# First layer of a fused convolution kernel on sums and differences of columns w and w+256, with a row transform 128 columns wide

## What is computed

```python
x = x + _L0_conv_ref(_gn(x), w_real, w_imag, b_real, b_imag)
x = x + _L1_conv_ref(_gn(x))
x = x + _L2_conv_ref(_gn(x), W)
x = x + _L3_conv_ref(_gn(x), weight)

def _L0_conv_ref(x, w_real, w_imag, b_real, b_imag):
    X = jnp.fft.rfftn(x, axes=(-2, -1), norm='backward')
    Xr, Xi = (jnp.real(X), jnp.imag(X))
    ...
    Yr = _rconv(Xr, wr) - _rconv(Xi, wi) + b_real[:, None, None]   # 3x3
    Yi = _rconv(Xr, wi) + _rconv(Xi, wr) + b_imag[:, None, None]
    return jnp.fft.irfftn(lax.complex(Yr, Yi), axes=(-2, -1), norm='backward')
def _L1_conv_ref(uvs):          # per channel: row sums, a 0/1 gate per row
    u, v = jnp.split(uvs, 2, axis=1)
    left_gate = relu(sign(einsum('bkmd,bkd->bkm', u, v.sum(axis=2))))[..., None]
    right_gate = relu(sign(einsum('bknd,bkd->bkn', v, u.sum(axis=2))))[..., None]
    return jnp.concatenate([left_gate * u, right_gate * v], axis=1)
```

## Time and profile before

| | |
|---|---|
| median of 3 runs | 4616.99 us (4616.7 to 4618.75) |
| profiled execution, its own time | 4618.31 us |
| its span | 4616.5 us |
| TensorE busy | 4235.7 us (92%), mean granted clock 0.959 of full speed |
| VectorE busy | 2761.5 us (60%) |
| ACT busy | 2639.8 us (57%) |
| GpSimd busy | 3.5 us in 22 instructions |

### The profile page before, as it was taken

How to read it: one execution, slowest core, us unless ns; L and a number is a source line. 1 busy time by engine, 2 the same in 40 slices (tenths; PEclk the granted TensorE clock), 3 DMA queues, 4 the chain that set the end, 5 groups by cost and what they waited for, 6 DMA issues and landing times.

```text
span 4616.5 us, 172871 instructions
## 1 busy us (share of the span) xinstructions
PE 4235.7 (92%) x60064; PEld 2295.8 (50%) x60064; DVE 2761.5 (60%) x9972; ACT 2639.8 (57%) x7597; POOL 3.5 (0%) x22
## 2 busy tenths in 40 slices
PE   4999899989999899998999989999899989888785
PEld 1555435555455544555445543555436553455441
DVE  1777727775377744777257771776727775377730
ACT  4456665547555565555655566555565556544453
POOL 0000000000000000000000000000000000000000
PEclk8999899999999999999999999999899999999987
DMA  7444666647665576665656566564766647544476
GB/s 203 110 120 114 166 162 175 175 132 183 159 177 175 139 171 163 176 175 147 162 160 176 168 160 165 159 175 145 170 157 177 177 135 183 144 120 124 107 183 183
DMA packets 437852, 732.96 MB, mean 159 GB/s; under 512 B 42544, under 2 KB 109296, under 8 KB 437232
## 3 DMA queue, kind: packets, MB, share of 16 engines
q1 hardware_dynamic: 416112, 688.51, 54.2%
q10 hardware_dynamic: 21248, 37.76, 4.1%
HBM read 323.98 MB, written 134.22 MB: 99 GB/s over the span
## 4 chain that ended last, share of the span: by engine, by line
PE 85%; DMA 6%; DVE 3%; issue 3%; SPq 2%; ACT 1%; ACTq 0%; DVEq 0%
PE ps L1358 26%; PE ps L1276 20%; PE ps L1261 19%; PE ps L1269 6%; PE ps L1285 5%; PE ps L1135 5%; DMA shared<-x 3%; DMA out<-x 2%; PE ps L1383 1%; DMA x<-x 1%; PE ps L1208 1%; PE ps L1181 1%; PE ps L1182 0%; SPq L401 0%; DVE shared L911 0%
## 5 line engine op out<-in xcount | busy, mean ns | idle before, releaser
L1358 PE MATMUL ps<-x,conv_s 64*32 64x512 f32 x12288 | 1398.5, 610 | 88.8 <-DMA shared<-x 83.6
L1358 PE MATMUL ps<-shared,conv_s 64*32 64x512 f32 x12288 | 1407.1, 609 | 0.0
L645 ACT ACTIVATE x<-ps,vec 128x256 f32 (+1 forms) x1024 | 491.3, 496 | 998.1 <-PE ps L1276 998.1
L1276 PE MATMUL ps<-hil,shared 128*128 128x256 f32 x4096 | 993.6, 386 | 0.0
L1276 PEld LDWEIGHTS ps<-hil,shared 128*128 128x128 f32 x4096 | 740.4, 190 | 273.8 <-issue 194.1
L911 DVE SCALAR_TENSOR_TENSOR shared<-xin,trig 128x256 f32<-128x256 f32 x2048 | 822.2, 440 | 57.3
L1358 PEld LDWEIGHTS ps<-x,conv_s 64*32 64x32 f32 x12288 | 428.0, 108 | 646.1 <-issue 581.6
L720 ACT ACTIVATE x<-ps,vec 64x512 f32<-64x512 f32 (+1 forms) x768 | 526.3, 685 | 340.7 <-PE ps L1358 331.1
L1261 PE MATMUL ps<-shared 32*32 32x512 f32 x16384 | 657.9, 602 | 0.0
L923 DVE COPY vsb<-ps 128x512 f32<-128x512 f32 x512 | 329.9, 686 | 545.9 <-PE ps L1261 545.9
L1358 PEld LDWEIGHTS ps<-shared,conv_s 64*32 64x32 f32 x12288 | 501.4, 108 | 196.6 <-issue 157.4
(11 more groups left out here) (175 smaller groups left out, 3366.5 us busy)
## 6 DMA issues: line engine op xcount, KB each, us to landing
shared<-x SPq DMA_DIRECT2D x680, 256.0 KB, 4.8
xin<-x SPq DMA_DIRECT2D x512, 256.0 KB
out<-x SPq DMA_DIRECT2D x512, 256.0 KB
shared<-x SPq DMA_DIRECT2D x128, 768.0 KB, 7.0
shared<-x SPq DMA_DIRECT2D x496, 128.0 KB, 3.5
shared<-t_strip SPq DMA_DIRECT2D x512, 96.0 KB, 3.7
shared<-x ACTq DMA_DIRECT2D x128, 256.0 KB, 4.3
x<-x SPq DMA_DIRECT2D x64, 256.0 KB, 9.1
```

The lines of the kernel that those rows point to most:

```text
L645: ins = nc.scalar.activation(split_in(strip_of(s))[:, q, :], split_in(ps[:, bank, :])[:, q, :], ACT.Identity, bias=v1(MEAN), accum_out=sum ...
L1276: mm = pe.matmul(split_in(ps[:, BY + 2 * odd + e, :])[:, int(q < 2), :], xt[:, e, q, :], hil[:, q, 0:HALF], start=False, stop=True, skip_g ...
L1358: mm = pe.matmul(ps[TM * cg:TM * cg + TM, banks[k], :], conv_s[rows, kw, kind, :], of, start=(kw == 0), stop=(kw == TAPS - 1), skip_group_ ...
```

## The change

- `xin` is split by GpSimd, behind the load: the upper 256 columns become x[w]-x[w+256], the lower ones x[w]+x[w+256], less twice the mean. VectorE no longer takes the mean off; it waits for `x_split` in place of the load. Cos and sin change sign from w to w+256, so a product by them turns sums into differences and back: planes are now four pieces of 128 columns with sums and two of 256 without.
- All of the first layer's values stay sums and differences, to `x1`. The row transform takes them to themselves: each of its four products covers 128 columns (`hil_s`). `over_half` keeps the old transform for the column sums.
- ACT evicts the lower half in two pieces of 128 columns, even and odd, with sums, and the upper half in one of 256 without. ACT makes the copy of V of the second strip, VectorE that of the first.
- The gates bring the columns back: GpSimd makes gate times the lower half plus offset (`lifts`, four slots), VectorE adds and subtracts gate times the upper half (`gate_low`, `gate_high`).
- Tables and `u` are scaled by one half; `u`, the column sums and the setup get their own sums and differences; sums and squares are doubled on the way to the gates.

```diff
-    hil_t = np.zeros((P, 4, HW_))
+    hil_t = np.zeros((P, HIL))
     for k in range(4):
         rows = split[k * P:(k + 1) * P]
         cols = n[1::2] if k < 2 else n[::2]
-        hil_t[:, k, :HALF] = hil[rows][:, cols]
-        hil_t[:, k, HALF:] = g[rows]
+        if k % 2 == 0:
+            hil_t[:, HALF * (k // 2):HALF * (k // 2 + 1)] = hil[rows][:, cols]
+            for half, sign in enumerate((1, -1)):
+                hil_t[:, HIL_S + P * (k + half):HIL_S + P * (k + half + 1)] = hil[rows][:, cols[:P]] + sign * hil[rows][:, cols[P:]]
+        hil_t[:, HIL_G + NG * k:HIL_G + NG * (k + 1)] = g[rows]
...
-            strip[s, h + 3 * C + ch, p] = row_out == 0
+                strip[s, h + C * k + ch, p] = 0.5 * f[row_out]
+            strip[s, h + 3 * C + ch, p] = 0.5 * (row_out == 0)
...
-    eye_mix[p, 0, AXS, p % TM] = 1.0
+    eye_mix[p, 0, AXS, p % TM] = 0.5
...
-DVE_B = 6
+DVE_B = 7
+POOL_B = 2
+LIFT_FREE = 4
...
-        hil = sb("hil", P, 4, HW_)
+        hil = sb("hil", P, HIL)
+        hil_lo = hil[:, 0:N].rearrange("p (k w) -> p k w", k=2)
+        hil_g = hil[:, HIL_G:HIL_S].rearrange("p (k g) -> p k g", k=4)
+        hil_s = hil[:, HIL_S:HIL].rearrange("p (k w) -> p k w", k=4)
...
+        lifts = [a[:, HALF * h:HALF * (h + 1)] for a in (colv, vs) for h in range(2)]
+        junk_d = xt[:, 1].rearrange("p a b -> p (a b)")
...
+            pool.sem_inc(gated, LIFT_FREE)
             with pool.Fori(0, B) as i:
+
+                pool.wait_ge(v_scaled, i + 1)
+                pool.sem_inc(s_pad, 1)
+                with pool.Fori(0, STRIPS // UNROLL) as j:
+                    for k in range(UNROLL):
+                        b = Steps(pool, p_steps, (i * STRIPS + j * UNROLL + k) * POOL_B)
+                        low, high = (halves(xin[:, k, :])[:, h, :] for h in range(2))
+                        pool.wait_ge(x_loaded[k], (i * (STRIPS // UNROLL) + j + 1) * 16)
+                        b.then(nc.gpsimd.tensor_tensor(high, low, high, ALU.subtract))
+                        pool.sem_inc(s_pad, 1)
+                        b.then(nc.gpsimd.tensor_scalar(low, low, v1(MEAN), 2.0, ALU.subtract, ALU.mult))
+                        nc.gpsimd.tensor_tensor(low, low, high, ALU.subtract).then_inc(x_split, 1)
...
+                pool.wait_ge(v_gates, i + 1)
+                for n in range(STRIPS):
+                    s = STRIPS - 1 - n
+                    pool.wait_ge(gated, gd(i, n - LIFT_FREE + 1))
+                    pool.sem_inc(s_pad, 1)
+                    for q in range(2):
+                        ins = nc.gpsimd.tensor_scalar(split_in(lifts[n % LIFT_FREE])[:, q, :], signs(x1[:, s, 1:1 + N])[:, 0, q, :], cols[:, 4, s:s + 1],
+                                                      gate_b[:, q, s:s + 1], ALU.mult, ALU.add)
+                    ins.then_inc(lifted, 1)
...
-                        ins = nc.scalar.activation(split_in(strip_of(s))[:, q, :], split_in(ps[:, bank, :])[:, q, :], ACT.Identity, bias=v1(MEAN),
-                                                   accum_out=sums[:, q, bass.ds(s, 1)])
-                    ins.then_inc(y_evicted, 1)
+                        nc.scalar.activation(signs(strip_of(s))[:, 0, q, :], signs(ps[:, bank, :])[:, 0, q, :], ACT.Identity, bias=v1(MEAN),
+                                             accum_out=sums[:, q, bass.ds(s, 1)])
+                    nc.scalar.activation(halves(strip_of(s))[:, 1, :], halves(ps[:, bank, :])[:, 1, :], ACT.Identity).then_inc(y_evicted, 1)
+
+                def copy_v(t):
+
+                    act.wait_ge(mixed, i * PAIRS + t + 1 + MIXED_CREDIT)
+                    act.wait_ge(turned, t0 + t * 2 + T_CREDIT)
+                    nc.scalar.activation(vsb[:, 1, :], ps[:, BV + 1, :], ACT.Identity).then_inc(v_copied[1], 1)
...
                 def step(t, odd, uses):
 
+                    copy_v(t)
                     for e in range(2):
                         evict(t * 2 - 2 + e, e, BY + 2 * (1 - odd) + e, 2 * (1 - odd) + e, uses)
                         turned_out(t * 2 + e, e)
                     squares(t * 2 - 2, 2 * (1 - odd), uses)
 
+                copy_v(0)
...
+                low, high = (halves(u[0:48, :])[:, k, :] for k in range(2))
+                c.then(V.tensor_tensor(high, low, high, ALU.subtract))
+                c.then(V.scalar_tensor_tensor(low, low, 2.0, high, ALU.mult, ALU.subtract))
                 V.tensor_copy(u[HP:HP + 48, :], u[0:48, :]).then_inc(v_u, 1)
-                V.tensor_scalar(u_sum, u[2 * C:4 * C, :], small[2 * C:4 * C, 1:2], None, ALU.mult).then_inc(v_zc, 1)
+                c.then(V.tensor_scalar(u_sum, u[2 * C:4 * C, :], small[2 * C:4 * C, 1:2], None, ALU.mult))
+                low, high = (halves(u_sum)[:, k, :] for k in range(2))
+                c.then(V.tensor_tensor(high, low, high, ALU.subtract))
+                V.scalar_tensor_tensor(low, low, 2.0, high, ALU.mult, ALU.subtract).then_inc(v_zc, 1)
...
-                trig_of = lambda a, q: split_in(trig[:, a, :])[:, q, :]
-
-                def make_planes(b, s, k, loads, pair):
-
-                    dve.wait_ge(x_loaded[k], loads * 16)
+                def make_planes(b, s, k, pair):
+
+                    dve.wait_ge(x_split, t0 + s + 1)
                     dve.wait_ge(mixed, i * PAIRS + pair - 1 + MIXED_CREDIT)
                     fg = lambda a: a.rearrange("p v a o -> p (v a o)")
-                    halves_in = lambda a, q: split_in(a)[:, q, :]
-                    b.did(V.tensor_scalar(xin[:, k, :], xin[:, k, :], v1(MEAN), None, ALU.subtract))
-                    b.then(V.scalar_tensor_tensor(fg(wst[:, wst_at(k)]), fg(mix_s[:, 1]), row_trig[:, 0, bass.ds(s, 1)], fg(mix_s[:, 0]), ALU.mult, ALU.add))
+                    b.did(V.scalar_tensor_tensor(fg(wst[:, wst_at(k)]), fg(mix_s[:, 1]), row_trig[:, 0, bass.ds(s, 1)], fg(mix_s[:, 0]), ALU.mult, ALU.add))
                     for a in range(2):
                         for q in range(2):
-                            ins = V.scalar_tensor_tensor(halves_in(planes[:, a, k, :], q), halves_in(xin[:, k, :], q), 1.0, trig_of(a, q),
-                                                         ALU.mult, ALU.mult, accum_out=gsum[:, 2 * a + q, bass.ds(s, 1)])
-                            if a == 0 or q == 0:
-                                b.did(ins)
+                            b.did(V.scalar_tensor_tensor(signs(planes[:, a, k, :])[:, 0, q, :], signs(xin[:, k, :])[:, 1, q, :], 1.0, signs(trig[:, a, :])[:, 0, q, :],
+                                                         ALU.mult, ALU.mult, accum_out=gsum[:, 2 * a + q, bass.ds(s, 1)]))
+                        ins = V.tensor_tensor(halves(planes[:, a, k, :])[:, 1, :], halves(xin[:, k, :])[:, 0, :], halves(trig[:, a, :])[:, 0, :], ALU.mult)
                         if a == 0:
+                            b.did(ins)
+                            b.settle(but=3)
                             b.did(V.scalar_tensor_tensor(fg(wst[:, wst_at(k)]), fg(mix_s[:, 2]), row_trig[:, 1, bass.ds(s, 1)], fg(wst[:, wst_at(k)]), ALU.mult, ALU.add))
                     ins.then_inc(planes_ready, 1)
 
-                def copy_v(s, e, pair):
+                def copy_v(pair):
 
                     dve.wait_ge(mixed, i * PAIRS + pair + 1 + MIXED_CREDIT)
-                    dve.wait_ge(turned, t0 + s - 1 + T_CREDIT)
-                    V.tensor_copy(vsb[:, e, :], ps[:, BV + e, :]).then_inc(v_copied, 1)
+                    dve.wait_ge(turned, t0 + pair * 2 - 1 + T_CREDIT)
+                    V.tensor_copy(vsb[:, 0, :], ps[:, BV, :]).then_inc(v_copied[0], 1)
...
-                            for f in range(2):
-                                copy_v(pair * 2 + f, f, pair)
+                            copy_v(pair)
...
                 dve.wait_ge(a_cols, 6 * i + 6)
+                dve.sem_inc(s_dve, 1)
+                low, high = (halves(colv)[:, k, :] for k in range(2))
+                c.then(V.tensor_tensor(high, low, high, ALU.subtract))
+                c.then(V.scalar_tensor_tensor(low, low, 2.0, high, ALU.mult, ALU.subtract))
...
+                c.then(V.tensor_scalar(sums[:], sums[:], 2.0, None, ALU.mult))
                 c.did(V.scalar_tensor_tensor(w1, edge[:], float(HALF), sums[:], ALU.mult, ALU.add))
                 c.then(V.scalar_tensor_tensor(w2, edge[:], float(HALF) / 2, sums[:], ALU.mult, ALU.add))
                 V.scalar_tensor_tensor(S, w1[:, 0, :], 1.0, w1[:, 1, :], ALU.mult, ALU.add, accum_out=v1(ST1)).then_inc(v_sums1, 1)
                 c.then(V.scalar_tensor_tensor(w2, w2, 2.0, edge[:], ALU.mult, ALU.mult))
-                c.then(V.tensor_tensor(Q, Q, w2[:, 0, :], ALU.add))
+                c.then(V.scalar_tensor_tensor(Q, Q, 2.0, w2[:, 0, :], ALU.mult, ALU.add))
...
+                c.then(V.tensor_scalar(B_, A_, -1.0, None, ALU.mult))
                 dve.sem_inc(s_dve, 1)
 
-                def gate(k):
-
-                    s = STRIPS - 1 - k
-                    for q in range(2):
```

(64 more changed lines are left out.)

46 lines of the change are left out of this document (27 added, 19 removed).

## The result

The changed kernel takes **4661.3 us** (median of 4 runs, 4655.71 to 4664.69), the kernel before 4617.62 in the same comparison (4 runs): a ratio of **1.0093**, 95% interval 1.0076 to 1.0111. It is slower by 0.9%. The prediction was 4392, faster by 5%, and its range ended at 4490.

A forecast was written before the change was run, and what follows sets the result against it. TensorE was taken as the bound. First-layer steps gave 180 and 44 us, small terms +12-6-2-3, in all 225: 4618.3-225-1.3 = 4392. Range for 8 in 10: 4320 to 4490.

The forecast's parts named there:

- Step 1: TensorE's row transform: four products of 128 columns take 1.05 us, 0.78 off the first hilbert and 0.68 off the second.
- Step 2: ACT in the first layer: its copy of the turned tile makes the second turn wait 0.63 us; step 9.27, 0.83 less.
- X: Start of the first turn in a two-strip step of the first layer; the second turn was forecast at X+2.15.
- Step 3: Between load and planes in the first layer: GpSimd's split takes 2.1 us per strip and is hidden, 1.04 us spare.
- S: Time of GpSimd's three split instructions per strip, taken as 2.1 us, with limits of 1.2 and 2.5.
- 7.7+S/2: First-layer step when the loop from load through split and planes to VectorE's copy sets it: 9.27 at S = 3.1.
- Step 4: Layer 2's gates: GpSimd's lifts are hidden by TensorE's products up to 1.3 us per strip, about 0.65 a piece.
- The start of the gates: Before layer 2: first three strips ready 0.7 us later, 6 in all; doubling the sums adds 0.2 per image.
- Rival A: VectorE and GpSimd shut each other out: first-layer step 9.6, 97 us more than forecast, 4489; chance 0.2.
- Rival B: GpSimd is the bound: slower from 1.55 us per split instruction; at a step of 12, 5085; chance 0.07.
- Rival C: ACT doesn't hold the second turn: first-layer step 8.64, 137 us less, 4255; chance 0.07.
- the signs of being wrong: TensorE waits before the first turn, planes beyond 3 us, GpSimd busy over 70% of first layer, layer 2's 81 us grow.

The follow-up runs named there:

- e5: The changed kernel with GpSimd keeping only the split's difference and VectorE taking the other two instructions into its planes: 4529.88 us, ratio 0.9807.
- e3: The changed kernel with GpSimd's middle split instruction cut to 16 of 256 columns and its lifts to 16 of 128: 4411.96 us, ratio 0.955.
- e4: The kernel before the change, with GpSimd computing on scratch, alone at the start and beside the first layer: 4630.95 us, ratio 1.0027.

## Why the prediction was wrong

**Step 1, TensorE: right.** Four products of 128 columns take 1.00 us from start to start (1854.84-1853.84 in e5), for the 1.05 made from the earlier trace rows.

**Step 2, ACT: right,** once the split is out of the way (e5): X+2.15, a wait of 0.62, and steps of 9.23 and 9.09 for 9.27.

**Step 3, GpSimd's split: the step that failed in the first layer.** S = 2.1 with an upper end of 2.5 was built from a fill as if a read cost what a write does, and as if VectorE stood still beside it. Measured: 2.9 with VectorE idle, 3.3 to 4.1 with VectorE at work. The first number alone would still have been hidden, as 2.9 is below 3.1: the low price hid how thin the margin was, and VectorE's company used it up. The formula 7.7+S/2 gives 9.35 to 9.75, where steps from 9.15 to 10.3 were seen; VectorE's planes, 3.1 us instead of 2.4, add the rest. The sentence "beyond 3.1 each us costs half" was good, the number put into it wasn't. The first layer won 8 to 16 us per image (13 in the mean) instead of 27, and 20.5 instead of 46 in the last: 124 us of the miss. The Trainium skill's figure for a two-input add (GPSIMD Engine Reference, 3.1) gave 0.56 for 256 columns as an estimate. The trace has 0.8 for it, so the page was nearer than the fill, and still too low.

**Step 4, gates.** Its threshold was right: up to 1.3 us per strip, 0.65 a piece, is hidden (1.27 is, 1.51 isn't). The price was not: 0.14 a piece from the fill, 0.47 to 0.54 measured alone and 0.71 to 0.86 in the mean beside VectorE. Here too the price alone stays under the limit, and the company crosses it. This term, put at nothing in the sum, cost 15.8 us in each of 8 images: 126 us. I had the number at which it decides, and no rival for it. The start of the gates lost 4 us per image where 0.9 was forecast, 25 more in all. About 1.9 us per image are a stall in L1411 that the trace calls issue and that the line had not before (L1330); no run explains it or took the rest apart.

124+126+25 = 275, and layer 3 gave 3 back: 272, for the 269 that were missed. That e3 came within 20 us is no luck: it takes away the first two of these and leaves the third.

**Rival A** has the right mechanism (in e4 VectorE's instructions went from 0.44 to 0.52 and from 0.69 to 0.91 in the mean). The rule of the Trainium skill behind it (SBUF — State Buffer, "Who interferes with whom") fits these numbers, though no run here shows that an engine waits for exactly one whole instruction of the other. Its sum of 4489 took the same low S, it lengthened only VectorE's planes and not GpSimd's split, and it let the split of strip 0 escape. That split doesn't: VectorE's dots run beside it, and it is the longer one above (4.1 against 3.3 us). **Rival B**, at 1.55 us per instruction, had its price right for one of the three (1.57) and half of it for the others. **Rival C** did not happen. That layer 2 could grow stood only among the signs of being wrong, and it did. Two more of those signs came, the wait before the first turn and planes beyond 3 us; the fourth didn't, as GpSimd was busy for 190.47 of 314.40 us (61%) of the first layer.

## What to carry to other kernels

Before moving work to an idle engine, time each form of instruction there, in the company it will have: a fill is no bound for an instruction that reads and computes, and a price measured with the neighbour idle can stay under a limit that the real one crosses. When a hidden step has a threshold (here 1.3 us per strip), give it a rival with a price of its own, since a small error there is paid once per strip. When part of the work goes to a third engine, what counts beside its rate is how far ahead of that engine's own queue it runs: 13 or 17 strips made 75 us.

## What the runs showed that I had not expected

GpSimd's tensor_scalar on 256 columns with a pointer and a constant takes 1.2 us from start to start with VectorE idle, half as long again as a subtraction of two tensors (0.8), and up to 2.87 with VectorE at work. Cutting a lift from 128 to 16 columns beside VectorE shortens it only from 0.71 and 0.86 to 0.58 and 0.72. ACT's 128-column Identity with pointers for scale and bias takes 0.50 on average, 0.38 with a pointer bias and a running sum.
